# Moving the centering of small weights from VectorE to ScalarE and GpSimd, and repeating the small attention weights by a matmul

## What is computed

```
h  = LN(x)
q, k = bf16(h @ Wq.T), bf16(h @ Wk.T)     # one head of 128
q, k = rope(q), rope(k)
s  = exp(q @ k.T / sqrt(128)), causal
o  = row sums of s                         # one number for each row
a  = relu(o * fc1_w + fc1_b) @ fc2_w.T + fc2_b        # 1 -> 16 -> 128
x1 = x + LN(a)
y  = relu(LN(x1) @ W1[1] + b1[1]) @ W2[1] + b2[1]     # 128 -> 256 -> 128
out = x1 + LN(y)
```

## Time and profile before

| | us |
|---|---|
| median of 3 runs | 117.16 |
| lowest and highest run | 116.64, 118.07 |
| span of the profiled execution | 115.7 |
| DVE, PE, ACT, POOL busy within the span | 87.0, 90.1, 77.1, 75.5 |

### The profile page before, as it was taken

How to read it: one execution, slowest core, us unless ns; L and a number is a source line. 1 busy time by engine, 2 the same in 40 slices (tenths; PEclk the granted TensorE clock), 3 DMA queues, 4 the chain that set the end, 5 groups by cost and what they waited for, 6 DMA issues and landing times.

```text
span 115.7 us, 1824 instructions
## 1 busy us (share of the span) xinstructions
PE 90.1 (78%) x406; PEld 51.2 (44%) x412; DVE 87.0 (75%) x332; ACT 77.1 (67%) x242; POOL 75.5 (65%) x129
## 2 busy tenths in 40 slices
PE   0069693599773499999988999998899989788940
PEld 0046431333421344535742764843674837436630
DVE  2891872999999996896899989399879482786522
ACT  4003335346995056999799969989979999663540
POOL 5589995956999559449559359519438459663460
PEclk9999999679999557999999999999999999999995
DMA  3983388302503000300300240300300303020033
GB/s 84 269 238 102 99 250 269 110 0 57 127 0 91 3 0 6 91 0 0 91 3 0 85 102 0 91 0 0 93 0 3 91 6 91 0 76 15 0 91 91
DMA packets 12127, 7.87 MB, mean 68 GB/s; under 512 B 911, under 2 KB 11222, under 8 KB 12118
## 3 DMA queue, kind: packets, MB, share of 16 engines
q1 hardware_dynamic: 12118, 7.77, 24.0%
HBM read 3.58 MB, written 2.10 MB: 49 GB/s over the span
## 4 chain that ended last, share of the span: by engine, by line
DVE 26%; PE 21%; POOL 16%; SPq 11%; ACT 10%; issue 8%; DMA 4%; POOLq 1%; DVEq 0%
POOL rstd L377 9%; PE net L650 7%; ACT score L431 6%; PE score L615 5%; DVE stats L457 4%; PE ring L638 4%; DMA qk_swap<-qk 4%; DVE xn L350 4%; DVE x L530 3%; POOL z L350 3%; ACT junk L441 3%; SPq L275 3%; POOL ve L376 3%; DVE rot L507 2%; PE ring L595 2%
## 5 line engine op out<-in xcount | busy, mean ns | idle before, releaser
L431 ACT ACTIVATE score<-score 128x1024 f32<-128x1024 f32 (+7 forms) x48 | 37.5, 783 | 6.3 <-PE score L618 4.8
L377 POOL TENSOR_TENSOR rstd<-ve,half_neg 128x4 f32<-128x4 f32 (+1 forms) x36 | 35.6, 989 | 3.0
L376 POOL TENSOR_SCALAR ve<-mv 128x4 f32<-128x4 f32 (+1 forms) x36 | 10.1, 280 | 28.3 <-DVE mv L460 18.4
L615 PE MATMUL score<-qk_r 128*128 128x512 bf16 (+3 forms) x75 | 21.0, 356 | 7.1 <-DVE qk_r L508 4.8
L601 PE MATMUL ring<-xT,wqk 128*128 128x512 f32 (+1 forms) x36 | 22.3, 737 | 2.7 <-ACT qk L393 1.2
L393 ACT ACTIVATE qk<-ring 128x512 bf16<-128x512 f32 (+1 forms) x16 | 9.0, 574 | 14.7 <-PE ring L601 14.7
L638 PE MATMUL ring<-zT,w_s 128*128 128x512 f32 (+1 forms) x36 | 17.2, 568 | 0.1
L441 ACT ACTIVATE junk<-net 128x128 bf16<-128x128 f32 x48 | 12.7, 285 | 6.2 <-PE net L650 4.1
L615 PEld LDWEIGHTS score<-qk_r 128*128 128x128 bf16 x80 | 7.2, 100 | 19.7 <-issue 11.5
L650 PEld LDWEIGHTS net<-w_s,hid 128*128 128x128 f32 x128 | 15.5, 192 | 0.6
L650 PE MATMUL net<-w_s,hid 128*128 128x128 f32 x128 | 15.7, 275 | 0.1
(11 more groups left out here) (62 smaller groups left out, 131.4 us busy)
## 6 DMA issues: line engine op xcount, KB each, us to landing
x_s<-x SPq DMA_DIRECT2D x7, 256.0 KB, 4.2
qk_swap<-qk SPq DMA_DIRECT2D x14, 128.0 KB, 2.4
out<-out_s SPq DMA_DIRECT2D x7, 256.0 KB, 2.2
table<-tables SPq DMA_DIRECT2D x4, 256.0 KB, 4.2
x_s<-x SPq DMA_DIRECT2D x2, 128.0 KB, 2.2
w_s<-w SPq DMA_DIRECT2D x2, 128.0 KB, 2.2
qk_swap<-qk SPq DMA_DIRECT2D x4, 64.0 KB, 2.6
out<-out_s SPq DMA_DIRECT2D x2, 128.0 KB, 1.8
```

The source lines that it names most:

```text
L376: own_chain.link(eng.tensor_scalar(ve[:, g, slot[k], t], mv[:, g, slot[k], t, 1], EPS, None, ALU.add))
L377: ready_r[k].done(eng.tensor_tensor(rstd[:, g, slot[k], t], ve[:, g, slot[k], t], half_neg[:, 0:tiles], ALU.pow), m)
L431: s_exp.done(eng.activation(score[i % 2][:, 0:width], score[i % 2][:, 0:width], ACT.Exp, scale=SCALE, accum_out=rows[:, g, s, j:j + 1]), i)
L615: mm = eng.matmul(score[i % 2][:, at:at + width], query, qk_r[:, g0 + c, 1, 0:width], start=True, stop=c < gb)
```

## The change

- The centering moves from DVE to ACT. A mean is taken by a Copy activation with the scale -1/128 and an accumulated output into a spare tile, and added by an Identity activation whose bias operand is that mean. center_w2 and center_b2 stand before the copy of k 2 on ACT (ahead of the first exp), center_fc2 before the copy of k 3.
- The split of b2 into three parts moves to POOL (split_b2, before rs1 6). Three one-row copies of the parts into b2_s stay on DVE, behind rope 4. b2_s holds one tile and the first matmul of y reads it repeated.
- fc2 and fc1 are loaded once, side by side into 17 rows (fc_f). POOL makes a 0/1 matrix (make_repeat, before rs1 2) from the identity, and PE multiplies by it before tr1 3 (repeat_fc), which gives the 17 rows four times, at partitions 0, 32, 64 and 96, in net bank 1. center_fc2 reads them there and writes the diagonal blocks of fc2_c.
- b2 is loaded into its three rows by one transfer. SP issues three small transfers instead of eleven, and W2 before W1.
- Zeros for b2_s are written by POOL at the start, zeros for fc2_c and the ones by DVE at the start. setup_small and setup_ffn are gone.

The diff, without declarations and semaphores:

```diff
--- before.py
+++ after.py
@@ -190,14 +190,18 @@
         table = sb("table", [P, 2, length], BF16)
         wqk = sb("wqk", [P, 2, P], F32)
         fc1 = sb("fc1", [P, 2], F32)
-        fc2 = sb("fc2", [P, TILES, P], F32)
+        fc_f = sb("fc_f", [INNER + 1, 2 + P], F32)
+        repeat = sb("repeat", [P, P], F32)
         w1_s = sb("w1_s", [P, HIDDEN], F32)
         b1_s = sb("b1_s", [P, HC], F32)
         w2_s = sb("w2_s", [P, HC, P], F32)
         b2_f = sb("b2_f", [P, P], F32)
...
+        spare = sb("spare", [P, TILES * P], F32)
+        w2_c = sb("w2_c", [P, HC, P], F32)
+        fc2_c = sb("fc2_c", [P, TILES, P], F32)
         means = sb("means", [P, 4], F32)
 
         x_s = sb("x_s", [P, n_groups, TILES, P], F32)
...
@@ -288,15 +296,13 @@
             load_x(eng, 3)
             load_table(eng, 1)
             load_x(eng, 4)
-            eng.wait_ge(s_zeroed, 2)
-            for j in range(TILES):
-                eng.dma_start(fc2[BLOCK * j:BLOCK * j + INNER + 1, j, :], fc2_wb).then_inc(s_fc2, 16)
-                eng.dma_start(fc1[BLOCK * j:BLOCK * j + INNER + 1, :], fc1_wb).then_inc(s_fc1, 16)
+            eng.dma_start(fc_f[:, 2:2 + P], fc2_wb).then_inc(s_fc, 16)
+            eng.dma_start(fc_f[:, 0:2], fc1_wb).then_inc(s_fc, 16)
+            eng.dma_start(w2_s[:, :, :], w2[EXPERT].rearrange("(c p) o -> p c o", p=P)).then_inc(s_w2, 16)
             eng.dma_start(w1_s[:, :], w1[EXPERT]).then_inc(s_w1, 16)
             eng.dma_start(b1_s[:, :], b1[EXPERT]).then_inc(s_w1, 16)
-            eng.dma_start(w2_s[:, :, :], w2[EXPERT].rearrange("(c p) o -> p c o", p=P)).then_inc(s_w2, 16)
-            for part in range(3):
-                eng.dma_start(b2_f[32 * part:32 * part + 1, :], b2[EXPERT:EXPERT + 1, :]).then_inc(s_b2, 16)
+            eng.wait_ge(s_zeroed, 1)
+            eng.dma_start(b2_f[0:96:BLOCK, :], b2[EXPERT:EXPERT + 1, :].to_broadcast([3, P])).then_inc(s_b2, 16)
 
...
@@ -357,6 +363,7 @@
         def _(eng):
             own_chain = Chain(eng, s_pool)
             eng.memset(half_neg[:, :], -0.5)
+            eng.memset(b2_s[:, :], 0.0).then_inc(s_blank_b2, 1)
             eng.memset(ident[:, :], 0.0)
             eng.memset(ident_b[:, :], 0.0)
             own_chain.link(eng.memset(later[:, :], 0.0))
@@ -367,7 +374,25 @@
             eng.affine_select(out=later[:, :], in_=later[:, :], compare_op=ALU.is_ge, fill=MASKED, base=0,
                               pattern=[[-1, P]], channel_multiplier=1).then_inc(s_const, 1)
 
+            def make_repeat():
+
+                eng.wait_ge(s_const, 1)
+                eng.tensor_copy(repeat[:, :].rearrange("p (j c) -> p j c", c=BLOCK),
+                                ident[:, 0:BLOCK].unsqueeze(1).to_broadcast([P, TILES, BLOCK])).then_inc(s_repeat, 1)
+
+            def split_b2():
+
+                eng.wait_ge(s_b2m, 1)
+                own_chain.link(eng.tensor_copy(b2_h[:, 0, :], b2_r[:, 0, :]))
+                own_chain.link(eng.tensor_tensor(b2_r[:, 1, :], b2_r[:, 0, :], b2_h[:, 0, :], ALU.subtract))
+                own_chain.link(eng.tensor_copy(b2_h[:, 1, :], b2_r[:, 1, :]))
+                eng.tensor_tensor(b2_r[:, 2, :], b2_r[:, 1, :], b2_h[:, 1, :], ALU.subtract).then_inc(s_b2p, 1)
+
             for name, m, *rest in ORDER:
+                if name == "rs1" and m == 2:
+                    make_repeat()
+                if name == "rs1" and m == 6:
+                    split_b2()
                 if name in ("rs1", "rs3", "rs4", "rs5"):
                     k = int(name[2])
                     g, j0, tiles = fronts[m] if k == 1 else backs[m]
@@ -403,7 +428,7 @@
                 if m >= 2:
                     made["fc2"].wait(eng, m - 2)
                 if m == 0:
-                    eng.wait_ge(s_fc1, 16 * TILES)
+                    eng.wait_ge(s_fc1, 1)
                 r = tiles * BLOCK
                 ins = eng.activation(h1T[0:r, m % 2, :], src[0:r, 0:P], ACT.Relu, scale=fc1[0:r, 0:1],
                                      bias=fc1[0:r, 1:2])
@@ -422,7 +447,44 @@
 
         @block.scalar
         def _(eng):
+            def center_w2():
+
+                eng.wait_ge(s_w2, 16)
+                for c in range(HC):
+                    eng.activation(spare[:, c * P:(c + 1) * P], w2_s[:, c, :], ACT.Copy, scale=-1.0 / P,
+                                   accum_out=means[:, c:c + 1]).then_inc(s_mean_w2, 1)
+                eng.wait_ge(s_mean_w2, HC)
+                for c in range(HC):
+                    eng.activation(w2_c[:, c, :], w2_s[:, c, :], ACT.Identity,
+                                   bias=means[:, c:c + 1]).then_inc(s_w2c, 1)
+
+            def center_b2():
+
+                eng.wait_ge(s_b2, 16)
+                eng.activation(spare[:, 0:P], b2_f[:, :], ACT.Copy, scale=-1.0 / P,
+                               accum_out=means[:, 3:4]).then_inc(s_mean_b2, 1)
+                eng.wait_ge(s_mean_b2, 1)
+                eng.activation(b2_r[:, 0, :], b2_f[:, :], ACT.Identity, bias=means[:, 3:4]).then_inc(s_b2m, 1)
+
+            def center_fc2():
+
+                eng.wait_ge(s_fc_made, 1)
+                fc2 = net[1][:, 1, :]
+                eng.activation(fc1[:, :], net[1][:, 0, 0:2], ACT.Copy).then_inc(s_fc1, 1)
+                eng.activation(spare[:, 0:P], fc2, ACT.Copy, scale=-1.0 / P,
+                               accum_out=means[:, 2:3]).then_inc(s_mean_fc2, 1)
+                eng.wait_ge(s_mean_fc2, 1)
+                for j in range(TILES):
+                    r = slice(BLOCK * j, BLOCK * (j + 1))
+                    eng.activation(fc2_c[r, j, :], fc2[r], ACT.Identity,
+                                   bias=means[r, 2:3]).then_inc(s_fc2c, 1)
+
             for name, m, *rest in ORDER:
+                if name == "k" and m == 2:
+                    center_w2()
+                    center_b2()
+                if name == "k" and m == 3:
+                    center_fc2()
                 if name == "exp":
                     g, j, s = rest
                     i = seg_no[(m, g, j, s)]
@@ -447,8 +509,8 @@
         def _(eng):
             own_chain = Chain(eng, s_dve)
             eng.memset(b2_f[:, :], 0.0).then_inc(s_zeroed, 1)
-            eng.memset(fc1[:, :], 0.0)
-            eng.memset(fc2[:, :, :], 0.0).then_inc(s_zeroed, 1)
+            eng.memset(fc2_c[:, :, :], 0.0).then_inc(s_blank, 1)
+            eng.memset(ones_b[:, :], 1.0).then_inc(s_ones, 1)
 
             def bn(k, m, src):
 
@@ -464,41 +526,6 @@
                                              mv[:, g, slot[k], j0:j0 + tiles, 0], -1.0, None, ALU.mult)
                 var[k].done(last, m)
 
-            def setup_small():
-
-                eng.memset(ones_b[:, :], 1.0)
-                eng.memset(b2_s[:, :, :], 0.0)
-                eng.wait_ge(s_fc2, 16 * TILES)
-                own_chain.link(eng.reduce_sum(means[:, 0:1], fc2[:, :, :], AX.XY))
-                own_chain.link(eng.tensor_scalar(means[:, 1:2], means[:, 0:1], 1.0 / P, None, ALU.mult))
-                for j in range(TILES):
-                    r = slice(BLOCK * j, BLOCK * (j + 1))
-                    last = eng.tensor_scalar(fc2[r, j, :], fc2[r, j, :], means[r, 1:2], None, ALU.subtract)
-                last.then_inc(s_fc2c, 1)
-
-            def setup_ffn():
-
-                eng.wait_ge(s_w2, 16)
-                own_chain.link(eng.reduce_sum(means[:, 2:4], w2_s[:, :, :], AX.X))
-                own_chain.link(eng.tensor_scalar(means[:, 0:2], means[:, 2:4], 1.0 / P, None, ALU.mult))
-                for c in range(HC):
-                    last = eng.tensor_scalar(w2_s[:, c, :], w2_s[:, c, :], means[:, c:c + 1], None, ALU.subtract)
-                own_chain.link(last)
-                eng.wait_ge(s_b2, 48)
-                own_chain.link(eng.reduce_sum(means[:, 2:3], b2_f[:, :], AX.X))
-                own_chain.link(eng.tensor_scalar(means[:, 3:4], means[:, 2:3], 1.0 / P, None, ALU.mult))
-                own_chain.link(eng.tensor_scalar(b2_f[:, :], b2_f[:, :], means[:, 3:4], None, ALU.subtract))
-
-                own_chain.link(eng.tensor_copy(b2_h[:, 0, :], b2_f[:, :]))
-                own_chain.link(eng.tensor_tensor(b2_r[:, 0, :], b2_f[:, :], b2_h[:, 0, :], ALU.subtract))
-                own_chain.link(eng.tensor_copy(b2_h[:, 1, :], b2_r[:, 0, :]))
-                own_chain.link(eng.tensor_tensor(b2_r[:, 1, :], b2_r[:, 0, :], b2_h[:, 1, :], ALU.subtract))
-                own_chain.link(eng.tensor_copy(b2_h[:, 2, :], b2_r[:, 1, :]))
-                for part in range(3):
-                    r = slice(32 * part, 32 * part + 1)
-                    last = eng.tensor_copy(b2_s[r, :, :], b2_h[r, part:part + 1, :].to_broadcast([1, TILES, P]))
-                last.then_inc(s_b2c, 1)
-
             def rope(n):
                 g, c, w, t0 = rope_part(n)
                 s_cos.wait(eng, n)
@@ -539,10 +566,13 @@
                     bn(1, m, lambda j: x_s[:, g, j0 + j, :])
                 elif name == "rope":
                     rope(m)
```

(35 more changed lines are left out.)

12 lines of the change are left out of this document (8 added, 4 removed).

## The result

| us | before | changed |
|---|---|---|
| median of 4 runs each | 116.9 | 118.67 |
| lowest and highest run | 116.13, 118.07 | 118.29, 118.68 |
| span of the profiled execution | 115.7 | 116.5 |
| x1 of back 0 starts | 39.22 | 39.93 |

The ratio is 1.0183 with a 95% interval of 1.0136 to 1.023: the changed kernel is 1.8% slower.

What follows compares the result with a forecast made beforehand. POOL's order up to rs3 0 was taken as the next bound: 2.0 + 0.8 - 0.35 - 1.2 + 0.45 = +1.7 us against 2.6 of slack, so x1 0 comes 0.9 earlier: 117.16 - 0.9 = 116.3 us, range 115.1 to 118.2.

Steps and rivals of the forecast that it cites:

- slack: POOL's rs3 0 ended at 36.53, x1 0 began at 39.22; a shift of 2.6 us means nothing is gained.
- table load: Rival: Identity on ACT needs another activation table, x1 0 comes 3.9 us later, 120.2 us; chance 0.03.
- center_fc2: Block on ACT before the copy of k 3: 1.6 us long, less the pause, 0.8 us late (0.4 to 1.3).
- rope 1: On DVE beside POOL's cos 2, which starts later: rope 1 ends at 21.1, 0.35 us earlier (0 to 1.25).
- clock: PE's pause before rope 1's scores shrinks to near 2.1 us, so the 2.4 GHz level stays: 1.2 us earlier.
- split_b2 and contention: Four split operations on POOL add 2.0 us; ropes 3 and 4 blocking POOL at cos 4 and split_b2 add 0.45.
- the clock falls all the same: Rival: PE's clock still drops, sum 2.9, x1 0 at 39.5, 0.3 late, 117.5 us; chance 0.25.
- make_repeat: One copy on POOL before rs1 2, at most 0.67 us, covered by 1.4 us before PE's transposes: 0.
- price of 0: center_w2 and center_b2 on ACT ahead of the first exponential, about 1.9 us, hidden by ACT's pauses: cost 0.

Runs made afterwards that it cites:

- W2 later: Changed kernel with center_w2 and center_b2 moved on ACT behind the copy of tr1 3, not ahead of the first exponential: 118.07 us, 1.012 to before.
- kept-busy kernel: Changed kernel with 14 dummy products on TensorE in its pause for rope 1: 116.99 us, 1.006 to before.
- third trace of before: The unchanged kernel before, traced in a third execution: 116.42 us, one run, span 114.6.
- three traces with the collision: Executions of the kernel before in which norm1b 6 on DVE ran beside cos 5 on POOL; spans 115.7, 114.6 and, with early dummy products, 114.6.
- the one with early products: Kernel before with 34 dummy products on TensorE ahead of the first transpose: 116.49 us, 1.002 to before.
- early-clock pair: Kernel before and changed kernel, each with 34 dummy products on TensorE ahead of the first transpose: 116.49 and 117.77 us.

## Why the prediction was wrong

Its frame held. POOL's order became the bound, x1 0 was released by POOL's rstd, slack was used up at 2.6, no table load was added, and the tail behind x1 0 was constant. The terms failed, as shifts of the end of rs3 0 against the trace that was read:

| term | predicted | measured |
|---|---|---|
| center_fc2, rope 1, clock: start of cos 3 | +0.8 −0.35 −1.2 = −0.75 | +1.25 |
| split_b2 and contention | +2.0 +0.45 = +2.45 | +0.43 +2.75 −1.07 = +2.11 |
| sum | +1.7 | +3.36 |

*TensorE's clock (−1.2, measured 0): the step that failed most.* It let the pause shrink to 2.1 us by an earlier rope 1 and the repeat matmuls, and left the start of the pause where it was. The repeat matmuls did hold tr1 3 back, from 16.44 to 17.08, but the work ahead of them was done 1.4 earlier than before: q 2 took 1.12 us and not 2.08, k 2 1.08 and not 1.83. So the last product before the pause ended at 17.74 (17.08 and 0.66), sooner than the 18.46 of before, while rope 1 ended only 0.13 earlier. The pause grew to 3.71, and the clock fell. The slow q 2 belongs to the execution that was read and not to the kernel before: the two later traces of before have 1.13 and 1.12, and W2 later, a form of the changed kernel, has 2.08. The granted clock reads 1.00 from 13 to 18 us whether q 2 is slow or fast, so the rows don't show what made it slow.

The length of the pause was only half of the error. In the trace of W2 later, with its slow q 2, the pause was 2.35 us, close to the 2.1 of the prediction, and the clock fell all the same, with q 3 at 2.00 us:

```profile
21.59 0.48 PE L657 MATMUL score<-qk_r 128*128 128x384 bf16 x1 [2.35 <-DVE qk_r L535]
...
22.50 2.00 PE L643 MATMUL ring<-xT,wqk 128*128 128x512 f32 x2
```

```profile
22.00:23.00 1.00, 1.00 (x5) 0.67 (x4) 0.00 (x0) 0.79 (x3) 0.82 (x2) 0.50 0.02 6
```

So the step from "2.1 is nearer to 1.64" to "the clock stays up" was wrong too, as far as 2.35 stands for 2.1. The worth of the clock was about right, by the kept-busy kernel (1.2 us by the ratios, 1.6 by the medians). The rival "the clock falls all the same" had this outcome and 117.5.

*center_fc2 (+0.8, measured about +1.2).* ACT's timeline of the changed kernel:

```profile
25.60 0.17 ACT L473 ACTIVATE fc<-net 128x2 f32<-128x2 f32 x1
...
26.05 1.51 ACT L479 ACTIVATE fc_c<-net,means 32x128 f32<-32x128 f32 x4
27.59 1.09 ACT L418 ACTIVATE qk<-ring 128x512 bf16<-128x512 f32 x2
```

From 25.60 to 27.56 the block took 1.96 us and not 1.6, for the four Identities came 0.38 us apart and not 0.26: that price was put together from a square's start-to-start time and a pointer's share, and the chain shows 0.36 for each and a link. Less the pause of 0.73 that is 1.2. The start of cos 3 shows 1.38 without rope 1. The rest of some 0.15 is tr1 4, whose transposes took 0.89 us and not 0.63 while the clock was still low, so that its copy, with the block right behind it, began 0.08 later though that of q 3 began 0.11 earlier. The 1.36 us of the earlier center_fc2 are the same thing undone.

*rope 1 (−0.35, measured −0.13 against the trace read).* Against the later traces of before, where it ended at 20.39 to 20.66, it is late by 0.6 to 0.9 (21.30): there q 2 and k 2 were fast, and cos 2 began between 17.32 and 17.67 and not at 18.71. In the changed kernel two things hold cos 2 until 18.31: the copy of k 2 behind the first block (17.50 to 18.08, where the third trace of before has 16.56), and POOL's own order, which ended norm1 4 at 18.21, where the trace read has 17.26. Of these 0.95 some 0.3 are make_repeat (0.29 us at 7.22), which the prediction put at nothing, and 0.5 one pair of norm operations (1.45 us at 13.34, 0.92 before). Then DVE's first rope operation stands under POOL's multiply:

```profile
19.47 1.37 DVE L534 TENSOR_TENSOR rot<-qk_swap,table 128x512 bf16<-128x512 bf16 x1 [2.53 <-DMA qk_swap<-qk]
20.88 0.42 DVE L535 TENSOR_TENSOR qk_r<-rot 128x512 bf16<-128x512 bf16 x1
```

The last of two (0.42) was the predicted kind; the first (1.37) was to be free. Moving the first block gave 0.4 at rope 1 and 0.2 at x1 0 in the traces, and nothing in the medians (W2 later), so its price of 0 was right within what these runs can tell.

*split_b2 and contention (+2.45, measured +2.11): right in sum, the parts not.* Four operations took 2.75 to 3.15 us, since they, and not only cos 4, met the rope operations: the one that ran with DVE idle (L389) took the 0.43 us of the prediction, the other three 0.63 to 0.75. rs1 6 to rs3 0 got the 1.07 back. It is the largest single cost of the change: with the split on DVE the time is 2.0 less. The estimate by the Trainium skill, GPSIMD Engine Reference (1.7 us), was lower still, but the advice of its section Engine selection, to keep elementwise work on VectorE, is what these runs bear out.

Together: 1.2 for the clock, 0.43 for center_fc2, 0.22 for rope 1 and 0.15 for tr1 4, less 0.34 for the split and its contention, are the 1.66 us by which 3.36 exceeds the forecast 1.7.

*The base.* The sum was made against one execution with a span of 115.7; the later ones had 114.1 and 114.6. It put 1.5 us around the span, where 1.7 to 2.1 are measured in each of the 16 traces whose own time is known, so that execution took an estimated 117.5 and the forecast for it, by its own sum, should have been 116.6. That is 0.3 us. Then 1.66 from the sum (3.36 less 1.7) give 118.3, the measured 118.29.

The size against before is thus two steps: the slack of 2.6 was real in the three traces with the collision (the one read first, the third and the one with early products), and absent in the one without, where rs3 0 itself ended 1.1 later (37.61); the changed kernel put 3.4 us (the two traces first read) to 3.9 us (the early-clock pair) on it.

## What to carry to other kernels

Work taken off the busiest engine is worth only what the next in-order chain lets through: 9 us of DVE's work were 2.7 us of time, and under 5 us of it put into that chain (1.96 and 2.75) turned this into a loss; the same work set into pauses that the timeline shows (3 us on ACT, the stretch behind rope 2 on DVE) made a gain of 1.2%, and of 2.3% with PE's clock kept up. A term that hangs on a pause being shorter needs both its ends followed, also the engine that stops sooner, and a row that shows what a pause of that length does. And before a sum of tenths is made, look at more than one execution: here two traces of one program had the bound on different engines.
